# Two sets of buffers for the split parts of q and k in the first stage of an attention and feed-forward kernel

## The reference

```python
q = split_heads(x @ Wq + bq); k = split_heads(x @ Wk + bk); v = split_heads(x @ Wv + bv)
scores = einsum('bhid,bhjd->bhij', q, k)
rel = einsum('bhid,pd->bhip', q, rel_key)          # p = 256
bias = take_along_axis(rel, clip(j - i + p - 1, 0, p - 1), axis=3)
logits = where(j <= i, (scores + bias) * scale, -inf)
attn = softmax(logits);  out = einsum('bhij,bhjd->bhid', attn, v) @ Wo + bo
x = x + layernorm(out)
h = silu(w1(n) * s1) * w2(n) * s2;  h = gelu(h1(h));  h = gelu(h2(h));  x = x + layernorm(w3(h))
```

## Time and profile before

| | |
|---|---|
| device time, median of 3 runs | 740.18 us (736.39 to 741.16) |
| the profiled execution's own time | 739.48 us |
| its span, first to last instruction | 737.4 us |
| mean granted clock of TensorE | 0.945 |
| busy: TensorE / ScalarE / VectorE / GpSimd | 644.0 / 572.1 / 540.2 / 247.7 us |
| first exponential of stage two starts | 108.99 us |

### The profile page before, as it was taken

The page is one execution under the profiler, slowest core; times in us unless marked ns, Lnnn a source line. Parts: engine busy times, 40 slices in busy tenths (PEclk is TensorE's granted clock), DMA queues, the critical chain, the costliest instruction groups (busy, mean ns, idle before and its releaser), DMA issues.

```text
span 737.4 us, 18944 instructions
## 1 busy us (share of the span) xinstructions
PE 644.0 (87%) x8066; PEld 467.7 (63%) x8066; DVE 540.2 (73%) x923; ACT 572.1 (78%) x660; POOL 247.7 (34%) x175
## 2 busy tenths in 40 slices
PE   4877569999999999999999999978799898998993
PEld 2433336676766766857667667655588687786682
DVE  5894787788687877786878777775677668588546
ACT  2784977988989889889898798786577868677573
POOL 2100180370640913706409128000271441731901
PEclk9988767999999999999999999997999999999997
DMA  7487424152241231521412314050300000000001
GB/s 229 110 224 225 133 63 111 35 132 66 50 114 36 73 94 35 128 70 50 106 46 70 96 34 116 24 166 2 100 1 1 0 1 1 1 29 0 5 25 59
DMA packets 39175, 52.82 MB, mean 72 GB/s; under 512 B 5656, under 2 KB 29640, under 8 KB 36680
## 3 DMA queue, kind: packets, MB, share of 16 engines
q1 hardware_dynamic: 39088, 51.58, 25.6%
HBM read 39.00 MB, written 11.81 MB: 69 GB/s over the span
## 4 chain that ended last, share of the span: by engine, by line
PE 53%; DVE 13%; ACT 12%; issue 5%; POOL 2%; DVEq 0%; ACTq 0%; POOLq 0%
PE p_o L1112 16%; PE p_s L1087 13%; PE p_z L1786 8%; PE p_z L1789 8%; DVE probs L1213 6%; ACT probs L1330 6%; PE p_s L1021 5%; POOL hid_lo L1707 1%; DVE res L1967 1%; ACT hid_hi L1890 1%; ACT o_acc L1339 1%; ACT even_b L1034 1%; ACT odd_b L1034 1%; PE p_o L1124 1%; DVE hid_lo L1991 1%
## 5 line engine op out<-in xcount | busy, mean ns | idle before, releaser
L1087 PE MATMUL p_s<-q_sb,k_sb 96*128 96x128 bf16 (+1 forms) x1600 | 172.1, 250 | 9.9 <-ACT probs L1330 4.7
L1330 ACT ACTIVATE probs<-p_s 128x1024 f32<-128x1024 f32 x160 | 156.7, 1017 | 19.9 <-DVE p_s L1222 10.8
L1112 PE MATMUL p_o<-probs,v_sb 128*32 128x128 f32 (+1 forms) x3200 | 159.9, 331 | 7.5 <-ACT o_acc L1339 4.4
L990 POOL TENSOR_SCALAR_AFFINE_SELECT even_b<-even_b 128x2048 f32<-128x2048 f32 x31 | 75.0, 2420 | 261.3 <-ACT even_b L1034 261.3
L1330 ACT ACTIVATE probs<-probs 128x1024 f32<-128x1024 f32 x128 | 133.5, 1055 | 35.7 <-DVE probs L1213 35.4
L1087 PEld LDWEIGHTS p_s<-q_sb,k_sb 96*128 96x128 bf16 x1600 | 113.8, 100 | 69.5 <-issue 29.5
L1213 DVE TENSOR_TENSOR probs<-p_s,even_b 128x1024 f32<-128x1024 f32 x96 | 114.9, 1219 | 16.6 <-PE p_s L1087 16.6
L1112 PEld LDWEIGHTS p_o<-probs,v_sb 128*32 128x32 f32 x3200 | 84.6, 111 | 41.0 <-issue 14.1
L1786 PE MATMUL p_z<-hid_hi,h_hi 128*128 128x512 f32 x256 | 102.0, 399 | 1.7 <-POOL hid_lo L1707 1.7
L1021 PE MATMUL p_s<-q_rows,rel_w 72*128 72x64 bf16 x2048 | 84.5, 197 | 20.1 <-DVE probs L1213 8.7
L1789 PE MATMUL p_z<-hid_lo,h_hi 128*128 128x512 f32 x256 | 100.9, 394 | 0.0
(11 more groups left out here) (182 smaller groups left out, 844.7 us busy)
## 6 DMA issues: line engine op xcount, KB each, us to landing
k_sb<-k_dram SPq DMA_DIRECT2D x48, 192.0 KB
q_sb<-q_dram SPq DMA_DIRECT2D x16, 576.0 KB
q_rows<-qr_dram SPq DMA_DIRECT2D x42, 192.0 KB
q_dram<-q_parts SPq DMA_DIRECT2D x12, 256.0 KB, 3.1
k_dram<-k_parts SPq DMA_DIRECT2D x12, 256.0 KB, 3.2
qr_dram<-q_turned SPq DMA_DIRECT2D x12, 256.0 KB, 3.4
x_all<-in_L_attn_x_dram SPq DMA_DIRECT2D x4, 512.0 KB, 4.2
every<-in_L_ffn_h_w_dram SPq DMA_DIRECT2D x2, 1024.0 KB, 8.4
```

Source lines behind the costliest of these rows:

```text
L990: nc.gpsimd.affine_select(out=far, in_=near, compare_op=ALU.is_ge, fill=0.0, base=-1 - r, pattern=[[0, QB], [-1, MCH * RCH]], channel_mult ...
L1087: last = nc.tensor.matmul(slot[:, c:c + n * BLK], k_sb[hg][:, h * S + j * BLK:h * S + (j + 1) * BLK], ap(q_sb[hg], at, [[HG * S, KROWS], [ ...
L1112: last = nc.tensor.matmul(p_o[32 * h:32 * h + 32, at:at + blocks * BLK], v_sb[hg][:, j, h * 32:(h + 1) * 32], probs[n % PBUFS][:, h, col * ...
L1330: nc.scalar.activation(to, got, ACT.Exp, scale=SCALE).then_inc(t_exp, 1)
```

## The change

The part buffers get a second set: q_parts, k_parts and q_turned are now pairs, and batch b uses set b % 2. The room for it is taken from a filler (STORED_ROOM) of the on-chip memory. m_parts of batches 0 and 1 lies in the room of these batches' tokens, which the layer norm has read by then; batches 2 and 3 use one buffer (m_late). The store semaphores are pairs as well. A buffer's next writer waits for the stores of the batch two before it (stored). At the end of stage one ScalarE and VectorE wait for the stores of batch 2, whose set lies in the room of stage two's first buffers; ScalarE waits for the shifts of batches 0 and 1 before its first copy of the fill.

SP loads only half 0 of the first unit in batch 1; half 1 follows in batch 2, behind the shift of batch 1. In bound, the wait for own moves from ahead of the first product to ahead of the first product that reads it.

```diff
-STORED_ROOM = 5184
+STORED_ROOM = 576
@@ buffers
+    early_parts = [sb(f"{n}0", [128, PARTS, S], BF16, one) for n in ("q_parts", "k_parts", "q_turned")]
     sb("stored_room", [128, STORED_ROOM], F32, one)
-    q_parts, k_parts = (sb(n, [128, PARTS, S], BF16, one) for n in ("q_parts", "k_parts"))
-    m_parts = sb("m_parts", [H, MPARTS, S], BF16, one)
-    q_turned = sb("q_turned", [128, PARTS, S], BF16, one)
+    q_late, k_late = (sb(f"{n}1", [128, PARTS, S], BF16, one) for n in ("q_parts", "k_parts"))
+    m_late = sb("m_late", [H, MPARTS, S], BF16, one)
+    turned_late = sb("q_turned1", [128, PARTS, S], BF16, one)
+    q_parts, k_parts, q_turned = zip(early_parts, (q_late, k_late, turned_late))
+    def m_parts(b):
+        if b >= 2:
+            return m_late[:, :, :]
+        return x_all[0:H, b * S:(b + 1) * S].bitcast(BF16).rearrange("h (m s) -> h m s", m=MPARTS)
+    def stored(eng, b, sems):
+        for done in sems:
+            eng.wait_ge(done[b % 2], (b // 2 + 1) * (16 * PARTS))
@@ sync_one, batch
             if b == 2:
-                sp.wait_ge(s_mst, 16)
+                sp.wait_ge(s_mst[0], 16)
                 for hg in range(2):
                     load_m(0, hg)
             if not first:
                 shift(b - 1)
             if b == 1:
-                for done in (s_qst, s_kst, s_rst):
-                    sp.wait_ge(done, 16 * PARTS)
+                stored(sp, 0, (s_qst, s_kst, s_rst))
                 sp.dma_start(q_rows[:, :], ...).then_inc(t_qr[0], 16)
-                for hg in range(2):
-                    load_k(0, hg)
-                    load_q(0, hg)
+            if b in (1, 2):
+                load_k(0, b - 1)
+                load_q(0, b - 1)
@@ vector_one and scalar_one, at their ends
+        stored(dve, B - 2, (s_qst, s_kst, s_rst))
+        stored(act, B - 2, (s_qst, s_kst, s_rst))
@@ scalar_one, turn_query
-            if b > 0 and part == 0:
-                act.wait_ge(s_rst, 16 * PARTS * b)
+            if b >= 2 and part == 0:
+                stored(act, b - 2, (s_rst,))
@@ scalar_one, batch
             if last_batch:
+                act.wait_ge(s_mst[0], 16 * 2)
                 for c in range(FIRST_BEFORE):
                     copy_act(act, "even", c)
-            if not first:
-                act.wait_ge(s_turned, b * PARTS)
-                act.wait_ge(s_qst, b * (16 * PARTS))
-                act.wait_ge(s_kst, b * (16 * PARTS))
-            nc.scalar.activation(q_parts[:, 0, :], qf[:, :], ACT.Identity).then_inc(s_hi, 1)
+            if b >= 2:
+                act.wait_ge(s_turned, (b - 1) * PARTS)
+                stored(act, b - 2, (s_qst, s_kst))
+            nc.scalar.activation(q_parts[b % 2][:, 0, :], qf[:, :], ACT.Identity).then_inc(s_hi, 1)
...
-            if not first:
-                act.wait_ge(s_mst, b * 16)
+            if last_batch:
+                act.wait_ge(s_mst[1], 16)
@@ tensor_one, bound
             pe.wait_ge(s_pos, b + 1)
-            pe.wait_ge(s_own, b + 1)
             for j in range(2):
                 ...
                 nc.tensor.matmul(p_tr[0:2 * GAP, c], k_sel[:, 1, :], qf[:, c], start=False, stop=False)
+                if j == 0:
+                    pe.wait_ge(s_own, b + 1)
                 nc.tensor.matmul(p_tr[0:2 * GAP, c], hneg[:, :], own[:, c], start=False, stop=True).then_inc(s_u, 1)
```

More of the change, by code:

```diff
@@ L284, in build @@
     s_turned = sem("s_turned")
-    s_rst = sem("s_rst")
+    s_rst = [sem(f"s_rst{p}") for p in range(2)]
     s_pos = sem("s_pos")
@@ L295, in build @@
     s_wabs, s_wany = sem("s_wabs"), sem("s_wany")
-    s_qst, s_kst, s_mst = sem("s_qst"), sem("s_kst"), sem("s_mst")
+    s_qst, s_kst, s_mst = ([sem(f"{n}{p}") for p in range(2)] for n in ("s_qst", "s_kst", "s_mst"))
     t_q = [sem(f"t_q{p}") for p in range(2)]
@@ L392, in shift @@
             sp.wait_ge(s_mr, b + 1)
-            sp.dma_start(ap(m_dram, b * (H * S), [[S, H], [DROW, MPARTS], [1, S]]), m_parts[:, :, :]).then_inc(s_mst, 16)
+            sp.dma_start(ap(m_dram, b * (H * S), [[S, H], [DROW, MPARTS], [1, S]]), m_parts(b)).then_inc(s_mst[b // 2], 16)
         def store(b, to, rows, part, got, done):
             sp.dma_start(ap(to, rows[0] * part + b * (H * S), [[S, H], [rows[1], HD], [1, S]]),
-                         got[:, part, :]).then_inc(done, 16)
+                         got[b % 2][:, part, :]).then_inc(done[b % 2], 16)
         def turned(b, part):
@@ L427, in sync_one @@
             turned(B - 1, part)
[L428 to L431, removed]
+        for b in (B - 2, B - 1):
+            stored(sp, b, (s_qst, s_kst, s_rst))
+        for p in range(2):
+            sp.wait_ge(s_mst[p], 16 * 2)
         sp.wait_ge(s_gap, B + 3)
@@ L510, in shift_rest @@
             dve.wait_ge(s_mneg, b * 2 + 2)
-            nc.vector.scalar_tensor_tensor(out=m_parts[:, 1, :], in0=p_tr[0:H, :], scalar=-1.0, in1=m_parts[:, 0, :],
+            nc.vector.scalar_tensor_tensor(out=m_parts(b)[:, 1, :], in0=p_tr[0:H, :], scalar=-1.0, in1=m_parts(b)[:, 0, :],
                                            op0=ALU.mult, op1=ALU.subtract).then_inc(s_mr, 1)
@@ L649, in turn_query @@
             act.wait_ge((s_hi, s_mid, s_low)[part], b * 2 + 1)
-            if b > 0 and part == 0:
-                act.wait_ge(s_rst, 16 * PARTS * b)
-            nc.scalar.activation(turned_view(q_turned, part), untouched_view(q_parts, part),
+            if b >= 2 and part == 0:
+                stored(act, b - 2, (s_rst,))
+            nc.scalar.activation(turned_view(q_turned[b % 2], part), untouched_view(q_parts[b % 2], part),
                                  ACT.Identity).then_inc(s_turned, 1)
@@ L696, in batch @@
                 act.wait_ge(s_u, b * 2 + j + 1)
-                nc.scalar.activation(m_parts[:, 0, j * 512:(j + 1) * 512], p_tr[0:H, j * 512:(j + 1) * 512],
+                nc.scalar.activation(m_parts(b)[:, 0, j * 512:(j + 1) * 512], p_tr[0:H, j * 512:(j + 1) * 512],
                                      ACT.Identity, scale=-1.0).then_inc(s_mneg, 1)
@@ L963, in room_free @@
             eng.wait_ge(s_turned, PARTS * B)
-            eng.wait_ge(s_qst, 16 * PARTS * B)
-            eng.wait_ge(s_kst, 16 * PARTS * B)
+            stored(eng, B - 1, (s_qst, s_kst))
         if m == 3:
-            eng.wait_ge(s_mst, 16 * B)
+            eng.wait_ge(s_mst[1], 16 * 2)
     def filled(eng, entry):
@@ L1334, in keep @@
             if u == 0 and hg == 0:
-                act.wait_ge(s_rst, 16 * PARTS * B)
+                stored(act, B - 1, (s_rst,))
             act.wait_ge(t_pv, u * SETS + (hg + 1) * EVEN)
```

14 lines of the change are left out of this document (7 added, 7 removed).

## The result

| | before | changed kernel |
|---|---|---|
| device time, median of 19 runs each | 739.24 us (734.91 to 741.61) | 732.53 us (729.75 to 735.34) |
| ratio, 95% interval | | 0.9919 [0.9903, 0.9934] |
| the profiled execution's own time | 739.48 us | 734.27 us |
| its span / what lies around it | 737.4 / 2.1 us | 732.5 / 1.8 us |
| first exponential of stage two | 108.99 us | 103.20 us |

The ratio is worth 6.0 us (4.9 to 7.2); 6.1 were forecast, and 733.6 us for the time. Between the two profiled executions 5.79 us come out ahead of the first exponential, 0.9 are given back behind it, and 0.3 lie outside the span: together the 5.2 us between them. One execution of an experiment (e1, its profiled one) ran at a mean granted clock of 0.56 and took 1021 us; nothing is read from it.

The account below looks back on a forecast made before the run. The prediction found ScalarE stalled 8.9 us in stage one by a full queue ahead of batch 1's stores. Its terms, 5.9 + 0.3 + 0.0 - 0.1 = 6.1 us, led to 733.6 us, range 730.5 to 738.

Parts of the forecast that it names:

- The stall, taken out: Stage one, batch 2: ScalarE's 8.88 us wait for a store goes; 5.9 us gained, with TensorE's bounds late next.
- rival 1: As summed, 731.5 to 735.5 us; main term 4.9 to 7.3 us with TensorE's clock in batch 2; chance 0.60.
- Batch 3, the copies: The fill's copies in batch 3 wait less for TensorE's products: 0.3 us gained, bounds 0 and 0.6.
- Rival 2: TensorE's clock stays up in batch 3 or rises early in batch 2: 730.3 to 731.7 us; chance 0.16.
- hangs together by compute alone and moves with it: From qf of batch 3 to the first exponential (108.99 us) everything moves with qf; only two small waits can shrink.
- Loads moved: Loading the first unit's second half behind batch 1's shift makes neither SP nor any landing late: worth nothing.
- Own waited for later: TensorE's moved wait for own in bound: 0 to 0.2 us in batch 3, taken as 0.0.
- Waits and addresses: Some ten more semaphore waits, found passed, cost 0.1 us (0 to 0.5); the buffers' new places cost 0.
- rival 3: Stage two gives part back, TensorE's clock rising 2 to 4 us later there: 735.5 to 737.5 us; chance 0.14.

Follow-up runs that it names:

- e1: The changed kernel with both halves of the first unit loaded in batch 1 and the old wait for own, so the two sets alone: 733.57 us, ratio 0.9927.
- e10: The changed kernel once more, unedited: 732.63 us, ratio 0.9934.
- e7: The changed kernel with the wait for own back ahead of the first product: 732.27 us, ratio 0.9916.
- e9: The kernel before, one set, both halves of the first unit loaded in batch 2, later wait for own, q's turn ahead of m_parts in batch 2: 730.57 us.
- e6: The changed kernel with the edits of e4 and e3 together: 730.99 us, ratio 0.9902.
- e3: The changed kernel with GpSimd's first mask held until VectorE has made own of batch 3: 731.89 us, ratio 0.9910.
- e5: The changed kernel with GpSimd's first mask held until VectorE has made both rests of batch 3: 733.44 us, ratio 0.9928.
- e1b: The same kernel as e1, the two sets alone, run again for a trace: 734.02 us, a single execution.
- e2: The kernel before, one set, with only the first unit's second half loaded in batch 2 instead of batch 1: 732.03 us, ratio 0.9912.
- e4: The changed kernel with ScalarE's last turn of q in batch 2 ahead of its two m_parts instead of behind: 730.95 us, ratio 0.9895.
- e11: The same kernel as e4, run again beside e10 on one chip: 731.22 us, ratio 0.9907.
- e8: The kernel before, one set, with the change's loads, the later wait for own and e4's turn: 732.34 us, ratio 0.9920.

## Why the prediction held, and where it did not

**The stall, taken out: right, 0.7 us too small.** The first split at 64.39, ScalarE's wait for p_tr, and TensorE's bounds as the next thing late all came as worked out. The term was 5.9 and measured 6.62. The rest is the clock: p_q to the last bound took 10.66 us and not the 11.88 of the trace of before, close to the 10.45 of batch 0 that stood as rival 1's upper side; p_q itself started 0.40 us later, so 0.8 us of the 1.2 are left at the bounds. Where the clock rises differs between executions: the changed kernel itself took 11.63 us for the same products in e10, and in e7 and e9 the first part of the shift (m_late, m_parts) ended 0.9 and 1.2 us later than here. So the 0.7 us is the luck of one execution, inside the range that rival 1 gave.

**Batch 3, the copies: the size right, in part by luck.** They wait 0.21 us instead of 0.57. The fall of the clock was forecast near 80.2 and came at about 80.6. But the prediction reckoned it as 3.0 us behind the last fp32 product, as twice in the trace of before, and that did not hold: here it came 4.4 us behind the last product of v (76.25), in the experiments 2.2 (e7, and there the copies wait 0.63 us) to 5.8 (e9), and in e6 the clock did not fall before TensorE's next fp32 products. The products of v ended a microsecond sooner than reckoned, and that made up for it. Rival 2, a clock that stays up in batch 3, did not come in the profiled execution. In e6 it did, where TensorE stood still for only 0.89 us ahead of the fill: its slices from 78 to 86 us have a granted clock of 1.00. The chain to the exponential was no shorter for it (25.90 us, as in e3, where the clock fell), and rival 2's 730.3 to 731.7 is not what the changed kernel took.

**The step that failed is the sentence that everything from qf of batch 3 to the first exponential "hangs together by compute alone and moves with it".** It does not. The 0.3 us by which the copies came closer to qf went to GpSimd as well as to ScalarE: GpSimd's first mask starts when the copies have made it, and it used to start 0.24 us after VectorE's own. Now it starts 0.08 us ahead of it. From qf to the end of k_rest it takes 15.13 us instead of 13.05. From k_rest on, 1.25 us come back, because before a mask also held up k's low part (2.47 us, now 1.22). The net loss is 26.52 - 25.69 = 0.8 us. The runs divide by this order: own first (before, e3, e5, e6, e7) 25.1 to 25.9 us; mask first (the changed kernel twice, e1b, e2, e4, e11, e8, e9) 26.5 to 27.0. In e2, e8 and e9, with one set and the old addresses, it is k_sel that the mask holds, so neither the second set nor its place in memory makes the loss. Where no wait fixes it, the order is that of instructions which start within 0.4 us of each other. That the k_rest of before took 3.35 us, nearly three times a pass, stood in its trace; the prediction did not ask why.

**So the sum was right partly by cancellation.** At qf 0.7 us more came than the term had. From qf on 0.3 us less time was forecast and 0.8 us more was taken, a miss of 1.1. Together 6.62 - 0.83 = 5.8 us at the first exponential, which was forecast at 102.9 and came at 103.20.

**Loads moved, at nothing: right for this change, but they are not without worth.** With the sets there they added nothing (e1 against the changed kernel: 0.9927 and 0.9919, intervals overlap). Alone they bring as much as the whole change (e2). The landing times were reckoned a little too late: batch 1's last stores behind half a unit of loads were to land at 67.0, and in e2 ScalarE goes on behind them at 65.67. The earlier trace rows gave 214 GB/s on average, which the prediction used for every stretch; the changed kernel moved 298 from 59 to 66 us (columns as there) and 228 from 45 to 73.

```profile
59.00:66.00 7.00, 3.46 (x11) 2.03 (x12) 6.83 (x11) 5.43 (x7) 0.00 (x0) 0.83 0.81 298
```

**Own waited for later, at nothing: right within what can be measured (e7).** The reason given was too short. In batch 3, where the lock holds own or k_sel, TensorE with the old wait stands 2.63 us (e1b) and 2.78 us (e2) for own; in the changed kernel the products ahead of the wait run meanwhile, from 82.70. In e1b VectorE then waits 0.32 us for the bounds, in the changed kernel not at all. But with and without it qf to exp is 26.52 us (e1b and the changed kernel): it is k's rest that sets the end there. In e2, where the clock was low for longer, the bounds come later still, and e8, with the later wait, has 26.61 us against 27.01; that 0.4 us is one execution each.

**Waits and addresses, 0.1:** not told apart. No run shows its price. Outside the span 1.8 us were left instead of 2.1; the kernels with two sets have 1.7 to 1.85 there and the one-set kernels e2, e8 and e9 2.1 to 2.2. What makes it is open, and the prediction had no term for these 0.3 us.

**Stage two (rival 3).** 629.3 us against 628.4 looks like 0.9 given back, and is within the 1.5 allowed. Over the experiments that distance lies between 625.3 (e2) and 628.8 (e1b) with no relation to what was edited, and in e10, the changed kernel itself, it is 626.8. So the 0.9 is within the scatter between executions. Rival 3's mechanism, a clock that rises later in stage two, is not there: it rose 11.3 us behind the first exponential before (120.3) and 11.6 us behind it now, at 114.8:

```profile
114.00:116.00 2.00, 2.00 (x27) 1.02 (x25) 0.84 (x2) 1.75 (x2) 0.00 (x0) 0.80 0.48 12
```

What sets this scatter of 4 us is open. The mean granted clock differs between the executions (0.943 to 0.956) and goes with it: of the changed kernel's 19 runs the slowest (735.34 us) has the lowest, 0.944, and the fastest (729.75) has 0.953. That it is the cause was not tested.

**What would be better.** With e4's turn the changed kernel measured 0.9895 and 0.9907; the one-set kernel e9 has 0.9895. They are 1 to 2 us under the changed kernel, with intervals that overlap. As far as these runs tell, the second set of buffers, some 18 KB in each partition, isn't needed for either the gain of the change or for what is on top of it.

## What to carry to other kernels

When a wait for a buffer goes, ask first which engine is late next and put its end into the sum: that gave the size here, and filling the wait that takes the stall's place (e4) gave the next 1.9 us. A stall on stores can be cured at either end, by a second buffer or by moving what stands ahead of the stores in the queue; try the cheaper one alone. And where a duration in the trace is two or three times that of its like, find what it collides with before shifting the stretch as a whole: an order of two engines that rests on 0.2 us is not kept.

## What the runs showed of the hardware

- A pass of 128x1024 fp32 on VectorE with both inputs in the on-chip memory (1.2 to 1.3 us alone) takes up to 3.4 us beside a mask of GpSimd that started first, ending 1.05 to 1.07 us behind it. The mask takes 2.36 us alone and 3.05 to 3.3 us behind one such pass. Passes that read TensorE's output memory keep their 1.21 us. A mask that starts during the pass for m_parts is held even so, and up to 4.42 us long (e5).
- An advance of the copies by 0.3 us turned the order of the two and cost 2.1 us up to the end of k_rest, of which 0.8 us were left at the first exponential.
- SP takes 0.5 to 0.65 us to issue most stores, and 2.5 to 3.5 us for the last three of batch 1 where both halves' loads stand ahead of them (before and e1b).
- After the last product of v in batch 3 the granted clock fell 2.2 (e7) to 5.8 us (e9) later in twelve profiled executions, all but e6; the rise in batch 2 moved the same chain of products between 10.66 and 11.63 us in two executions of one kernel.
